# Rotary keys and queries of the second half of a batch: one projection and a transfer between partitions in place of two projections

## The reference, cut to what matters

```
q = proj(layernorm(x), Wq, bq)          # 32 rows, 16 heads of 8
k = proj(ctx, Wk, bk)
v = proj(ctx, Wv, bv)
q = q * cos + rotate_half(q) * sin      # rotate_half: [-x2, x1] of the two halves of a head
k = k * cos + rotate_half(k) * sin
attn = softmax(q k^T * Hd ** -0.5)      # 64 x 64 per row and head
out  = (attn v) Wo + bo
x = x + tanh(g) * out
```

## Time and profile before

| what | us |
|---|---|
| median of 3 runs | 275.29 |
| lowest and highest run | 274.83, 276.19 |
| span of the profiled execution | 274.8 |
| PE busy | 253.9 (92% of the span) |
| DVE, ACT, POOL busy | 190.7, 164.6, 131.0 |

### The profile page before, as it was taken

One profiled execution on the slowest core, in us unless ns is written; L12 is line 12 of the kernel. 1 busy time (PEld: TensorE's weight loads), 2 busy tenths in 40 slices (PEclk: granted clock), 3 DMA queues, 4 the chain that ended last, 5 costly groups with the idle time before them and its releaser, 6 DMA issues.

```text
span 274.8 us, 6251 instructions
## 1 busy us (share of the span) xinstructions
PE 253.9 (92%) x2152; PEld 196.4 (71%) x2152; DVE 190.7 (69%) x494; ACT 164.6 (60%) x384; POOL 131.0 (48%) x207
## 2 busy tenths in 40 slices
PE   8999999999899989999999999979998784989886
PEld 6655376666577868999999999665785442766675
DVE  3898688888988763253222223885769989999993
ACT  2369985666488654675566667473445793354453
POOL 4566579999402403218992220275066633353230
PEclk9999999999999998999999999999999999799999
DMA  6999000000000209776777771000000000000111
GB/s 191 379 348 403 13 4 2 2 4 0 2 2 4 76 20 377 300 289 265 296 300 291 292 290 63 2 1 1 4 0 0 0 0 2 0 19 23 38 39 38
DMA packets 12191, 30.11 MB, mean 110 GB/s; under 512 B 1024, under 2 KB 5248, under 8 KB 12032
## 3 DMA queue, kind: packets, MB, share of 16 engines
q1 hardware_dynamic: 12160, 29.71, 28.5%
HBM read 9.71 MB, written 1.05 MB: 39 GB/s over the span
## 4 chain that ended last, share of the span: by engine, by line
PE 64%; DVE 20%; issue 7%; ACT 5%; POOL 2%; DVEq 0%; POOLq 0%
PE ps L1403 12%; PE ps L1414 12%; PE ps L1252 6%; DVE s_region L294 4%; PE ps L1226 4%; PE ps L1239 4%; PE ps L1159 3%; DVE s_region L1090 3%; PE ps L1542 3%; PE ps L1150 2%; DVE s_small L1095 2%; PE ps L1262 2%; PE ps L1151 2%; PE ps L1344 2%; DVE s_small L237 2%
## 5 line engine op out<-in xcount | busy, mean ns | idle before, releaser
L631 ACT ACTIVATE s_region<-ps,s_region 128x128 f32<-128x128 f32 x144 | 40.8, 371 | 21.8 <-PE ps L1403 21.8
L960 DVE SCALAR_TENSOR_TENSOR s_ctxT<-ps,s_region,s_ctxT 128x64 f32 x72 | 18.1, 281 | 43.8 <-PE ps L1414 43.8
L1403 PE MATMUL ps<-s_region 128*128 128x128 f32 x288 | 38.0, 276 | 0.3 <-issue 0.3
L1414 PE MATMUL ps<-s_region 128*128 128x128 f32 x288 | 37.9, 275 | 0.0
L1403 PEld LDWEIGHTS ps<-s_region 128*128 128x128 f32 x288 | 34.9, 192 | 0.7 <-issue 0.7
L1414 PEld LDWEIGHTS ps<-s_region 128*128 128x128 f32 x288 | 35.0, 192 | 0.2 <-issue 0.2
L420 POOL COPY s_region<-s_xt 128x64 f32 x72 | 14.8, 234 | 32.3 <-PE ps L1403 24.5
L574 ACT COPY s_region<-ps 128x512 f32<-128x512 f32 x32 | 17.2, 592 | 16.2 <-PE ps L1239 16.2
L830 DVE TENSOR_REDUCE s_small<-ps 128x16 f32<-128x1024 f32 x16 | 19.6, 1224 | 9.7 <-PE ps L1226 9.7
L1599 PE MATMUL ps<-s_region 128*128 128x352 f32 x64 | 21.1, 469 | 5.3 <-DVE s_region L1090 3.7
L301 POOL TENSOR_TENSOR s_region<-s_region,s_small 128x704 f32<-128x704 f32 (+2 forms) x11 | 14.6, 1330 | 22.0 <-DVE s_region L294 21.7
(11 more groups left out here) (230 smaller groups left out, 528.7 us busy)
## 6 DMA issues: line engine op xcount, KB each, us to landing
s_region<-s_wall SPq DMA_DIRECT2D x36, 514.0 KB, 3.0
s_wall<-wall SPq DMA_DIRECT2D x8, 514.0 KB, 9.3
s_par<-par SPq DMA_DIRECT2D x1, 1280.0 KB, 10.5
s_x<-x SPq DMA_DIRECT2D x2, 512.0 KB, 6.8
out<-s_x SPq DMA_DIRECT2D x6, 128.0 KB, 1.8
s_region<-ffn SPq DMA_DIRECT2D x1, 560.0 KB, 3.6
s_ctxT<-ctxT SPq DMA_DIRECT2D x2, 256.0 KB, 4.0
s_ctxT<-ctxT SPq DMA_DIRECT2D x1, 512.0 KB, 6.7
```

Of the source, the lines that this page charges most:

```text
L631: ins = act.activation(hg[j % 3][:, c, :], ps[:, j % 3, RPT * S * c:RPT * S * (c + 1)], ACT.Gelu, bias=wbuf[j % 6][:, FF + FC * D + c:FF + ...
L960: dve.scalar_tensor_tensor(row, ps[:, 4 + j % 2, S * k:S * k + S], w, row, ALU.mult, ALU.add).then_inc(m["acc_done"], 1)
L1403: ins = mm(ps[:, j % 3, RPT * S * c:RPT * S * (c + 1)], w[:, P * c:P * c + P], xg[j % 4], start=True, stop=True)
L1414: ins = mm(ps[:, 4 + j % 2, 0:RPT * S], w[:, FF + D * c:FF + D * c + D], hg[j % 3][:, c, :], start=(c == 0), stop=(c == FC - 1))
```

## The change

Keys of groups 2 and 3 and queries of groups 2 and 3 (rows 16 to 31) get one product each. ACT copies it out with its bias (`keys_kept`, `late_projection`), SP then copies its partitions into a second buffer with partners exchanged, 8 transfers of 16 partitions (32 KB) for each group, and POOL multiplies by cos and sin and adds (`late_rope`). The key transfers are issued ahead of the expert weights, the query transfers behind them. PE's transposes of input groups 2 and 3 move behind the first scores. On ACT `keys_kept` stands ahead of `x_transposed`. On PE `values(6)` stands ahead of the query projections.

```diff
+            for i in range(2):
+                sp.wait_ge(m["k_raw"], i + 1)
+                rotate(kraw[i], "k_rotated")
             for e in range(E):
                 sp.dma_start(wall[:, e, :], a["wall"][e]).then_inc(m["ld_wall"], 16)
+            for i in range(2):
+                sp.wait_ge(m["q_raw"], i + 1)
+                rotate(qraw[i], "q_rotated")
...
+            def rotate(z, done):
+
+                for d in range(HD):
+                    sp.dma_start(z[1][d:P:HD], z[0][d ^ (HD // 2):P:HD]).then_inc(m[done], 16)
...
+            def late_rope(n, raw, dst):
+
+                pool.wait_ge(m["q_rotated" if n >= 2 else "k_rotated"], 256)
+                for z, table in zip(raw, ("cos", "sin")):
+                    pool.tensor_tensor(z, z, pc(table).unsqueeze(1).broadcast_to([P, 8, S]), ALU.mult).then_inc(m["q_turned"], 1)
+                pool.wait_ge(m["q_turned"], 2 * (n + 1))
+                pool.tensor_tensor(dst, raw[0], raw[1], ALU.add).then_inc(m["late_rope"], 1)
...
+            bias_rows()
+            late_keys(0)
+            late_keys(1)
+            late_queries(0)
...
-            late_queries(2)
             bias_added(0)
+            head_blocks(2)
             bias_added(1)
-            head_blocks(2)
+            late_queries(1)
             bias_added(2)
-            late_queries(3)
+            head_blocks(3)
             bias_added(3)
-            head_blocks(3)
...
             normalise(act, 0, TILES // 2, m["xn_a"], 1)
-            x_transposed(0)
-            x_transposed(1)
...
+            keys_kept(0)
+            keys_kept(1)
+            x_transposed(0)
+            x_transposed(1)
             values_kept(4)
             values_kept(5)
...
-            project(2)
-            project(3)
+            late_key_project(0)
+            late_key_project(1)
             values(4)
             values(5)
...
+            turn_inputs(0)
+            turn_inputs(1)
+            values(6)
+            for g in range(2):
+                pe.wait_ge(m["tr1_used"], g + 1)
+                project(2 + g)
+            values(7)
...
-                mm(ps[:, 2 * g, :], pc("wq0"), cols, start=True, stop=True)
-                mm(ps[:, 2 * g + 1, :], pc("wq0r"), cols, start=True, stop=True).then_inc(m["proj"], 1)
+                mm(ps[:, 2 * g, :], pc("wq0"), cols, start=True, stop=True).then_inc(m["proj"], 1)
...
             keys_queries(0)
+            turn_inputs(2)
             late_project(2)
+            turn_inputs(3)
+            keys_queries(1)
             late_project(3)
-            keys_queries(1)
```

More of the change, by code:

```diff
@@ L157, in build @@
         qraw = [[carve(24064 + 1024 * i + 512 * j, 8, S) for j in range(2)] for i in range(2)]
+        kraw = [[carve(26112 + 1024 * i + 512 * j, 8, S) for j in range(2)] for i in range(2)]
         bout, bvrep, borow = carve(23584, D), carve(23712, P), carve(23840, P)
@@ L358, in head_blocks @@
             def head_blocks(g):
-                pool.wait_ge(m["rope_sum"], g + 1)
+                pool.wait_ge(m["late_rope"], g - 1)
                 pool.wait_ge(m["s_done"], 4 * (g - 1))
@@ L366, in _, with late_keys, late_queries @@
             pool.wait_ge(m["hmask_ready"], 2)
-            for r in range(G4 + 2):
+            def late_rope(n, raw, dst):
[4 more added lines that the diff above has]
+                pool.tensor_tensor(dst, raw[0], raw[1], ALU.add).then_inc(m["late_rope"], 1)
+            def late_keys(i):
+                late_rope(i, kraw[i], kT[:, 8 * (2 + i):8 * (3 + i), :])
+            def late_queries(i):
+                late_rope(2 + i, qraw[i], qT[:, 8 * (2 + i):8 * (3 + i), :])
+            for r in range(4):
                 if r in (1, 2):
@@ L549, in late_projection, with keys_kept @@
             def late_projection(g):
[L551 to L555, removed]
+                act.wait_ge(m["proj"], 6 + g - 1)
+                act.activation(qraw[g - 2][0].rearrange("p b s -> p (b s)"), ps[:, 2 * g, :], ACT.Identity,
+                               bias=pc("bias0")[:, 0:1]).then_inc(m["q_raw"], 1)
+            def keys_kept(i):
+                act.wait_ge(m["proj"], 2 + i + 1)
+                act.activation(kraw[i][0].rearrange("p b s -> p (b s)"), ps[:, i, :], ACT.Identity,
+                               bias=pc("bias0")[:, 2:3]).then_inc(m["k_raw"], 1)
+            keys_kept(0)
+            keys_kept(1)
+            x_transposed(0)
+            x_transposed(1)
             values_kept(4)
@@ L803, in _ @@
                     ln_stats(dve, st, 8 * (r - 1), 8 * r)
-                col = COL["bias0"][0] + (2 if r < G4 else 0)
-                dve.wait_ge(m["proj"], r + 1)
+                if r == 2:
+                    dve.wait_ge(m["rope_sum"], 1)
+                    dve.wait_ge(m["hmask_ready"], 2)
+                    for j in range(4):
+                        dve.tensor_scalar(kbd[0][:, j, :], kT[:, 0:8, :].rearrange("p b s -> p (b s)"), hmask[:, j:j + 1], None,
+                                          ALU.mult).then_inc(m["kbd_first"], 1)
+                    normalise(dve, TILES // 2, 12, m["xn_a_late"], 2)
+                col = COL["bias0"][0] + (2 if r < 2 else 0)
+                dve.wait_ge(m["proj"], r + 1 if r < 2 else r + 3)
                 if r >= 2:
@@ L811, in _ @@
                         pc(table).unsqueeze(1).broadcast_to([P, 8, S]), ALU.add, ALU.mult).then_inc(m["rope_half"], 1)
[L812 to L816, removed]
-                                          ALU.mult).then_inc(m["kbd_first"], 1)
-                if r == 3:
-                    normalise(dve, TILES // 2, TILES, m["xn_a_late"], 2)
+            normalise(dve, 12, TILES, m["xn_a_late"], 2)
             def scores(u):
```

57 lines of the change are left out of this document (24 added, 33 removed).

## The result

| | before | after |
|---|---|---|
| median of 4 runs, us | 275.74 | 286.53 |
| lowest and highest, us | 274.83, 276.77 | 285.68, 290.04 |
| profiled execution, us | | 286.81, span 285.0 |

The ratio is 1.035, with a 95% interval of 1.029 to 1.041. The forecast was 281.8 us: slower was right, and 286.53 lies 1.2 us above the range.

A forecast was written before the change was run, and what follows sets the result against it. It took PE, busy 253.9 of 274.8 us, with waits through ACT and a tight POOL. Tile 12's +7.5 less 0.98 won back gave +6.5, so 281.3, plus 0.5 for the median: 281.8 us, range 279.3 to 285.3.

The forecast's parts named there:

- The first stretch: PE and ACT to 34 us: the 3.4 us saved go into waits, 1.6 us more; first probabilities transposed at 34.4.
- The transfers: SP's sixteen query transfers: from 33.3 us, 0.38 us per issue and 2.0 us landing, all landed by 41.4 us.
- My rival of slow transfers: Query transfers: stride-8 issues take 0.54 us or more and landing 3.0 us, giving 285.3 us and above; 8%.
- The weights ahead in the queue: Eight expert weights ahead of the query transfers, issued from about 25 us, land by 38 to 39 us, adding nothing.
- POOL's work behind the landing: On POOL: 3.8 + 1.28 us from landing to first bias, then 31.1 us until `head_blocks(3)` ends at 77.6 us.
- T: When POOL ends the first bias, `bias_added(0)`: forecast 46.5 us, against 37.7 before.
- Where the stall goes: From POOL's late bias to PE: third `weigh_values` +4.4 us, tile 12's scores +7.5, less 0.98 won back: +6.5.
- Past 95 us: PE's rows behind tile 12's delayed scores: the same rows, shifted, with no wait differing.
- Outside the span: End of the sum: 281.3 us for a profiled execution, plus only 0.5 us to reach the median, 281.8.
- The clock rival: PE's clock falls behind idle stretches, costing up to 1.7 us behind the first or last: 283.5 us; 14%.
- the long stall: PE's idle stretch at about 44 us, some 3 us; a clock fall there is covered by POOL's later chain.
- The "not slower" rival: At ACT's first late copy: saved products bring late queries forward, T 39.1, below the deciding 40.0; 274.4 us; 5%.

The follow-up runs named there:

- the wait for eight alone: Against the kernel after, the first late query rotation waits for its own eight transfers, not all sixteen; 287.36 us, ratio 1.036.
- both together: Against the kernel after, each query group waits for its own eight transfers and expert weights are issued behind the query transfers; profiled run 282.85 us.
- the neighbouring partitions: Against the kernel after, each transfer takes 16 neighbouring partitions instead of every eighth, giving wrong rotation partners; 288.53 us in one run.
- The version that gained: Against the kernel after, query transfers ahead of weights, split waits, first bias earlier, PE reordered, blocks moved to ACT and DVE; 272.60 us, 0.991 of before.

## Why the prediction was wrong, by its own steps

**The first stretch** was right within half a microsecond. `values(6)` waited 2.21 us (2.3), scores started at 26.24 (26.0), the first late query was copied out at 33.8 (33.3), and the first probabilities were transposed at 34.81 (34.4). The saved products did go into waits. One wait was missed: the keys' transfers, which were to cost POOL arithmetic alone, landed by 29.5 us and not by 27, and POOL waited 1.15 us for them.

**The transfers: the step that failed**, in a size. I took 0.38 us for an issue with its pause, from the smallest transfer shown (a store of 64 KB), with 0.54 as the upper bound (a copy between partitions). It is 0.63: both bounds were too low, and 0.38 was itself the lowest row with its pause, while the low bound left the pause out. The row chosen was the nearest in bytes; bytes turned out not to matter (0.59 us for 16 KB and for 32 KB, 0.47 to 0.60 for 256 KB), and the row nearest in kind, SBUF to SBUF, would have come closer, though it too lies below (0.54 with its pause against 0.63). The sum was 33.3 + 16 x 0.38 + 2.0 = 41.4; measured is 33.83 + 10.33 up to the start of the sixteenth issue + 1.86 = 46.02. Of the 4.6 us too little, 0.5 is the start, 4.25 the issue and -0.14 the landing. My rival of slow transfers, with 8%, is the one in whose range the time fell. It asked for 0.54 us or more and a landing of 3.0; the first half came true and the second did not, and the reason that it gave, the stride of 8, was not the reason: without the stride an issue takes as long.

The landing was right where it counted: 1.86 us for the sixteenth, forecast 2.0. The first eight, behind the expert weights, took 4.8 to 7.5 us, which the sixteenth's issue covered. The Trainium skill, "DMA: Bandwidth & Descriptors", "Anatomy of one DMA", gives 2.0 us and a term for bytes, for transfers issued on another path; the trace agrees for copies with no loads ahead of them. The Trainium skill, in the section "Issuing engines are not separate DMA queues" of the same page, calls the time to start a transfer usually small beside the transfer itself. Here it is not: one issue takes 0.59 us beside a landing of 1.9, and since the issues stand one behind another, sixteen take 10.1 to 10.9 us. The Trainium skill, "Perfetto Trace Analysis", 'What "DMA-bound" means', names an issuing sequencer that is solid with DMA instructions as a bound of its own; SP's row of 10.92 us for 16 is that.

**The weights ahead in the queue** landed up to 43.0 us (31.9 + 11.1), not by 38 to 39, since the keys' issues took 10 us and held them up. This hid behind the slow issue: the weights moved alone gained nothing, and the wait for eight alone gained 1.05 us, but both together gained 5.7.

**POOL's work behind the landing** was right. It took 5.0 us to T (3.8 + 1.28). T + 31.1 = 82.2, and tile 12's scores start at 82.18. In the runs in which POOL sets the time the same sum holds: 44.59 + 31.1 = 75.7 for one transfer a group, measured 75.65.

**Where the stall goes.** I counted 0.98 us as won back, since DVE would be ahead. At 87.55 PE still waits 0.67 us for DVE, so 0.31 is won back: +12.04 at tile 12 becomes +11.7. The step that failed is that DVE's statistics would be done during the stall. They stand in DVE's list behind a later `add_out` (at 82.40 us here, 70.67 before), so the stall put them off with all the rest. And with the clock at 0.50 PE caught up so much less that only 0.24 us were left to wait when POOL released tile 12.

**Past 95 us** I said that no wait differs. That is not so for the clock: before had it at 0.50 to 0.66 between 102 and 106 us, behind a wait of 0.47 us, and after does not have it at the same products, behind the same wait. Windows of before, then of after at the same work:

```profile
102.00:104.00 2.00, 2.00 (x6) 0.50 0.57 226
104.00:106.00 2.00, 2.00 (x11) 0.66 0.98 387
```

```profile
114.00:118.00 4.00, 4.00 (x26) 1.00 0.84 332
```

That gives back about 0.5 x 2 + 0.34 x 2 = 1.7 us, and 11.7 - 10.2 = 1.5 is what the spans show. The record speaks against the change as its cause, since executions of before differ in just this amount. Of the 41 that were timed beside the experiments, 12 have a mean granted clock of 0.987 or 0.988, as the profile has, and a median span of 274.75 us; 18 have 0.993 or 0.994 and a median of 273.2. They have no traces, so that it is this fall which they lack is inferred from its size. If so, the span of 274.8 us that I started from held an extra fall, and 285.0 - 273.2 = 11.8 is close to the 11.7 at tile 12.

**Outside the span.** I took nothing. Each profiled run here is 1.7 to 1.9 us longer than its span (286.81 and 285.0 for after), so the profile of before was of a run of about 276.6 us, not of its fastest. The error of 4.7 us is thus 4.6 for T, -0.9 for what stands behind T (0.67 not won back, 1.5 given back), and +1.0 for what lies outside the span and the median.

**The clock rival**, 14% (the 1.7 us of the earlier trace rows are what the lower level cost, not how long it lasted): its fall behind the first idle stretch did not come in after, but came with the neighbouring partitions and cost 2.0 us there. The fall behind the long stall did come in after, 0.50 from 48 to 56 us, and cost nothing, since POOL's chain was later, as forecast. With the queue empty and a wait for each group a fall (there behind 2.57 us at 34.45) was no longer covered and cost 1.4 us. The fall ahead of the end, behind a wait for POOL at tile 12, came in two other kernels: behind 3.56 us with the first bias moved, and behind 2.45 us with one transfer a group. By their windows (PE's busy time in each, times what the clock lacked to 1.00) these cost some 4.4 and 3.4 us, an estimate, and more than the 1.7 that I had put. The long stall's fall in windows of after:

```profile
48.00:50.00 2.00, 0.00 (x0) 0.50 0.00 0
...
54.00:56.00 2.00, 2.00 (x11) 0.50 0.00 0
```

**The "not slower" rival** needed T below 40.0. That figure counted on the 0.98 us; with 0.31 won back it is 70.14 + 0.31 - 31.1 = 39.4. The run without transfers has 41.24 and, at the same clock, is 1.8 us longer than before, which fits (41.24 - 39.4 = 1.8); no kernel with sixteen transfers and POOL's order of after reaches it.

## What to carry to other kernels

When many small transfers replace arithmetic, count issues, not bytes: one engine's issues stand one behind another, and the price of one is taken from a row of the same kind of transfer, not of the same size, and with a margin, for here that row was low too. Ask which work stands behind the waiting instruction on its engine: free transfers alone did not make the change pay, nor did moving the bias alone. The version that gained made these moves, and those on PE, ACT and DVE, all at once, so what each is worth is not shown. And here the removed products were worth their time only once the order on the engines behind PE was changed with them.

## What the runs showed of the hardware

An SBUF-to-SBUF issue on SP took 0.59 us in the median for 16 partitions, strided by 8 or neighbouring, for 16 KB and for 32 KB, and 0.47 to 0.60 for 128 partitions and 256 KB; a load of the expert weights took 0.43 to 0.46 in the median, and a copy out of `wall` 0.49, though each moves 514 KB. Why a copy of 16 partitions takes 0.1 us more than these is open. In every kernel with 32 such issues or more the longest took 1.08 to 1.69 us, with the weights ahead of them or behind; why is open too. The clock was less regular than I had taken it: the idle 2.2 to 2.6 us of the first stretch stood in after and in eight of the experiments, and a fall followed in three of them (one transfer a group, neighbours, both edits of the queue); and 0.7 us of idleness ahead of the same matmul instructions was followed by a fall in one of two kernels that differ only in where POOL, 175 us earlier, adds the first bias. Executions of one and the same kernel differ too: 18 of before have a mean clock of 0.993 or 0.994, 12 have 0.987 or 0.988 and span 1.5 us more in the median. An idle stretch in a profile tells that a fall can come, not that it will.
